# Three changes of place in a hand-ordered scan: one convolution step, the cumulated sums, the residual scaling

## The chip, the core and the metric

One core of one Trainium2 chip. TensorE (PE) multiplies, VectorE (DVE), ScalarE (ACT) and GpSimd (POOL) work element by element, SyncE (SP) issues transfers. The metric is the device time of one execution in microseconds (us).

## The reference

A picture batch of 8 x 128 x 32 x 32 goes through three blocks: attention over the 1024 positions, a state-space scan over the 1024 tokens of each batch element, and a mixture of 8 experts of which each token takes two. The part that the change touches is the scan block. Cut to what matters:

```python
x = x + conv_attention(group_norm(x))
t = tokens(x)
u = rmsnorm(layernorm(t))
z, xBC, dt = split(u @ W_in)                    # 256, 320 and 8 columns
xBC = silu(sum(shift(xBC, k) * conv_w[:, k] for k in range(4)) + conv_b)
xs, Bm, Cm = split(xBC)                         # 256, 32, 32
dt = softplus(dt + dt_bias); dA = exp(dt * -exp(A_log))
state = state * dA + (dt * xs) outer Bm         # one step per token, 8 heads
y = state . Cm + Dp * xs
t = t + layernorm(t) + rmsnorm(y * silu(z)) @ W_out
t = t + experts(layernorm(t))
```

## The kernel before

The kernel has three stages: attention over the eight batch elements, then eight scans (one per batch element, `scanned`), then the experts. Each engine has its own written program; they meet only through semaphores.

A scan handles the 1024 tokens of batch element b in 8 chunks of 128 tokens. Work item n = 8 b + c is chunk c of scan b. In the text "mixed(8)" in a scan means the item of that number counted from the scan's own first chunk, so 8 is the first chunk of the next scan. What one chunk does:

- PE: `decay(n+2)` multiplies the row factors into banks 4 and 5; `out_product(n-2)` is the output projection (L969); `output_rows` (L948, L953, L960) makes y of the chunk; `increments` (L934) runs in chunk 0.
- ACT: `decays(n+2)` takes the exponential of the decay banks (L1341).
- DVE: `mixed(n+1)` multiplies the decays by the inner products (L1805, two inputs in SBUF), `output(n-3)` adds the scaled product into X (L1832), then the chunk's y is gated by z (L1865), `mean_square(n-2)` follows (L1822).
- POOL: `operand` (L531), `root(n-2)`, which takes the power -1/2 of the mean square and releases `output` (L570), and its own parts.

Between these lie the parts that prepare the scans to come. They stand in one list per engine, `pe_parts`, `act_parts`, `dve_parts` and `pool_parts`: which part, how many batch elements ahead, and in which chunk. A place c means after the first step of chunk c on that engine, c + 0.5 the chunk's end, c - 0.25 its start. `slot_of` puts every part of scan 0 one chunk later, at most at 7.5. Parts two elements ahead run in scans 0 to 5, those one ahead in scans 0 to 6.

The parts that matter here:

- The convolution of group g has a first tap on ACT (`tap`, L1272), which reads PE's product of that group, and three steps on DVE, ("conv", (g, k)) for k = 1, 2, 3 (L1713), each adding a shifted row from PSUM to `cacc`. Groups 0 and 1 are xs, group 2 is B and C. The last step raises `m_conv_ready`. Silu on ACT (L1284, L1289) follows in the next scan, where also the gates are multiplied on PE and put through silu on ACT (L1295).
- `softplus` on DVE (L1735 to L1743, two halves) ends with `dec_a` and raises `m_dt_ready`.
- `cumulate` on PE (L881 to L883) sums `dec_a`. It waits for `m_dt_ready` and, as it writes into banks that conv (1,3) reads, for `m_conv_ready` of group 1.
- `exponents` on DVE (L1753 to L1757) reads those sums; `factors` on ACT (L1325, L1328) follows, then PE's first gates, and SP sends the rows through DRAM.
- `shortcut` on ACT (L1258) scales X of one tile of 128 tokens by an instruction; eight make a batch element. Its result is first needed by `output` in the next scan.
- `weighted` on POOL (L561) multiplies xs by the end weights in two parts; the second stands in chunk 6 behind a wait for mixed(7). `decayed` on POOL (L551) stands in chunks 4 and 5. A part on POOL waits for the mix of its chunk first.

Of the kernel before, what the change touches and what calls it, by code (L numbers as in the profile page):

```python
# [16 lines left out]
def hybrid_kernel(nc, x, x_tok, wqk, bqk, wv, bv_rows, wo2, bo, ident, fold, group_mean,  # L17
# [21 lines left out]
    NT = N // P  # L39
# [15 lines left out]
    with ExitStack() as ctx:  # L55
# [598 lines left out]
        def _(pe):  # L654
# [318 lines left out]
            def scan(b, u, first, last):  # L973
                for c in range(NT):
# [31 lines left out]
                    elif c == 7:  # L1006
# [5 lines left out]
            pe_parts = [(gates, (0, 0), 1, 0), (gates, (0, 1), 1, 0), (gates, (1, 0), 1, 0.5), (gates, (1, 1), 1, 0.5), (turn_x, (0,), 1, 2), (turn_x, (1,), 1, 2), (turn_normed, (), 2, 2.5),  # L1012
                        (inner_products, (), 1, 2.5), (group, (0, 0), 2, 3.5), (group, (0, 1), 2, 3.5),
                        (steps, (0, 4), 2, 3.5), (turn_b, (), 1, 3.5), (steps, (4, NT), 2, 4), (group, (1, 0), 2, 4.5),
                        (group, (1, 1), 2, 4.5), (group, (2, 0), 2, 5.5), (group, (2, 1), 2, 5.5), (cumulate, (), 2, 6.5)]

            def pieces(b, slot):
                for part, of, ahead, at in pe_parts:
# [151 lines left out]
        def _(act):  # L1170
# [173 lines left out]
            def scan(b, u, first, last):  # L1344
                for c in range(NT):
# [12 lines left out]
                    elif c == 5:  # L1358
# [3 lines left out]

            act_parts = [(silus, (), 1, 0.5), (normed, (), 2, 1.5), (gather_x, (), 1, 2),
                         (high, (), 2, 2.5), (tap, (0,), 2, 3.5), (gather_b, (), 1, 3.5), (steps, (), 2, 4),
                         (shortcut, (0, 4), 1, 4), (tap, (1,), 2, 4.5), (softplus, (), 2, 4.5), (tap, (2,), 2, 5.5),
                         (shortcut, (4, NT), 1, 5.5), (factors, (), 2, 7)]

            def pieces(b, slot):
                for part, of, ahead, at in act_parts:
# [92 lines left out]
        def _(dve):  # L1462
# [228 lines left out]
            def front(b, u):  # L1691
# [74 lines left out]
                def inner():  # L1766
# [13 lines left out]

            dve_parts = [("conv", (2, 2), 1, -0.25), ("conv", (2, 3), 1, 0), ("ends", (), 1, 1), ("low", (), 2, 2.75),
                         ("inner", (), 1, 3), ("conv", (0, 1), 2, 4), ("conv", (0, 2), 2, 4), ("conv", (0, 3), 2, 4),
                         ("steps", (), 2, 4.5), ("conv", (1, 1), 2, 5), ("conv", (1, 2), 2, 5),
                         ("softplus", (0,), 2, 5.5), ("softplus", (1,), 2, 5.5), ("conv", (1, 3), 2, 6),
                         ("exponents", (), 2, 7), ("conv", (2, 1), 2, 7)]

            def second_front(slot):

# [335 lines left out]
```

## Time and profile before

| what | us |
|---|---|
| median of 3 runs | 956.29 |
| lowest and highest run | 955.75, 958.93 |
| the profiled execution | 954.08 |
| its span, first to last instruction | 952.3 |
| PE busy | 858.4 (90%) |
| DVE busy | 724.0 (76%) |
| ACT busy | 503.3 (53%) |
| POOL busy | 290.8 (31%) |
| all 72 convolution steps on DVE (L1713) | 91.8 |
| all 64 mixed on DVE (L1805) | 85.4 |

The profiled execution's times are those from which single instructions are read; the runs are what the change is measured against. Busy shares are means over three stages. A line of the timeline gives start, duration, engine, source line and operation; a bracket at its end gives how long the engine sat idle before it and what released it.

### The profile page before, as it was taken

How to read it: one execution, taken by the hardware profiler on the slowest of the kernel's cores; microseconds unless marked ns; L12 is line 12 of the kernel's file. 1: busy time of each engine (PE TensorE's matmuls, PEld its weight loads, DVE VectorE, ACT ScalarE, POOL GpSimd, SP SyncE). 2: the span in 40 equal slices, each digit the busy share in tenths (PEclk: the TensorE clock that was granted, in tenths of full speed). 3: DMA queues.
4: the chain of work that ended last, by engine and by line, in shares of the span. 5: the costliest groups of instructions: out<-in, count | busy, mean ns of one | idle time of the engine just before them, and what ended most of it. 6: DMA issues, size and time to landing. Idle time of an engine off the chain costs nothing.

```text
span 952.3 us, 18728 instructions
## 1 busy us (share of the span) xinstructions
PE 858.4 (90%) x7086; PEld 670.9 (70%) x7086; DVE 724.0 (76%) x1959; ACT 503.3 (53%) x740; POOL 290.8 (31%) x264
## 2 busy tenths in 40 slices
PE   3788999999998869898989899899789999999997
PEld 2555556656665758686868777776578898888887
DVE  2867677678767686868687787977968889888885
ACT  1524455455557457566575757464335544555453
POOL 0026110110010236354545454647530333033300
PEclk9979999999999879899999999999899999999999
DMA  5641011011100303213030303041000000000001
GB/s 150 192 143 23 1 23 23 1 23 23 23 1 0 77 4 74 48 31 71 8 76 3 78 1 78 1 96 50 2 1 1 24 23 24 1 23 23 24 2 44
DMA packets 30888, 36.07 MB, mean 38 GB/s; under 512 B 4560, under 2 KB 24912, under 8 KB 30800
## 3 DMA queue, kind: packets, MB, share of 16 engines
q1 hardware_dynamic: 29648, 30.68, 13.2%
q10 hardware_dynamic: 1152, 4.19, 1.2%
q8 instruction: 57, 0.93, 0.4%
q14 instruction: 31, 0.25, 0.1%
HBM read 21.50 MB, written 4.98 MB: 28 GB/s over the span
## 4 chain that ended last, share of the span: by engine, by line
PE 58%; DVE 27%; ACT 7%; issue 5%; POOL 2%; SPq 0%; DMA 0%; DVEq 0%; POOLq 0%; ACTq 0%
PE ps L1047 7%; PE ps L715 6%; DVE cacc L1713 5%; DVE acc L1997 5%; PE ps L702 4%; PE ps L794 3%; PE ps L969 3%; PE ps L796 3%; PE ps L669 3%; PE ps L795 3%; PE ps L674 2%; PE ps L691 2%; PE ps L905 2%; PE ps L684 2%; PE ps L919 2%
## 5 line engine op out<-in xcount | busy, mean ns | idle before, releaser
L1997 DVE SCALAR_TENSOR_TENSOR acc<-ps,comb,acc 128x128 f32<-128x128 f32 x512 | 139.8, 343 | 16.2 <-PE ps L1047 15.6
L1400 ACT ACTIVATE hid<-ps,b_f 128x512 f32<-128x512 f32 x128 | 87.2, 687 | 112.2 <-PE ps L796 112.1
L1047 PEld LDWEIGHTS ps<-w_f,hid 128*128 128x128 f32 x1024 | 130.6, 191 | 19.5 <-ACT hid L1400 8.0
L1047 PE MATMUL ps<-w_f,hid 128*128 128x128 f32 x1024 | 136.8, 277 | 5.0 <-ACT hid L1400 4.5
L1570 DVE TENSOR_REDUCE nmax<-ps 128x1 f32<-128x1024 f32 x64 | 78.1, 1220 | 29.7 <-PE ps L674 29.4
L1713 DVE SCALAR_TENSOR_TENSOR cacc<-ps,cw,cacc 128x1023 f32<-128x1023 f32 (+5 forms) x72 | 91.8, 1275 | 9.4 <-ACT cacc L1272 7.7
L1341 ACT ACTIVATE dcy<-ps 128x1024 f32<-128x1024 f32 x64 | 65.2, 1018 | 62.4 <-PE ps L919 62.3
L570 POOL TENSOR_TENSOR srs<-sve,neg_half 128x1 f32<-128x1 f32 x64 | 58.4, 912 | 117.7 <-DVE gram L1822 117.6
L1187 ACT ACTIVATE probs<-ps,nmax 128x1024 f32<-128x1024 f32 x64 | 71.3, 1113 | 39.2 <-DVE nmax L1570 36.5
L1805 DVE SCALAR_TENSOR_TENSOR dcy<-dcy,g_sb 128x1024 f32<-128x1024 f32 x64 | 85.4, 1334 | 0.3
L702 PEld LDWEIGHTS ps<-id_f,probs 128*128 128x128 f32 x512 | 59.0, 142 | 33.0 <-issue 23.3
L1193 ACT ACTIVATE pt<-ps 128x512 f32<-128x512 f32 x64 | 38.1, 595 | 75.4 <-PE ps L702 74.9
L702 PE MATMUL ps<-id_f,probs 128*128 128x128 f32 x512 | 68.8, 277 | 8.8 <-ACT pt L1193 6.7
L518 POOL TENSOR_TENSOR rs<-bve,neg_half 128x16 f32<-128x16 f32 x8 | 23.2, 2903 | 166.0 <-DVE bve L1618 166.0
L969 PE MATMUL ps<-y_w 128*128 128x256 f32 x256 | 69.4, 395 | 4.9 <-DVE X L1832 4.3
L1575 DVE COPY pt<-ps 128x512 f32<-128x512 f32 x64 | 43.8, 685 | 27.3 <-PE ps L702 27.0
L715 PE MATMUL ps<-pt,v_f 128*64 128x512 f32 x256 | 63.8, 613 | 0.0
L1865 DVE TENSOR_TENSOR y_w<-ps,zs 128x256 f32<-128x256 f32 x64 | 26.9, 420 | 47.8 <-PE ps L960 43.5
L794 PE MATMUL ps<-uh,w_h 128*128 128x512 f32 x128 | 61.1, 478 | 0.0
L1272 ACT ACTIVATE cacc<-ps,cb,cw 128x1024 f32<-128x1024 f32 x24 | 28.9, 1205 | 56.8 <-PE ps L796 56.8
L969 PEld LDWEIGHTS ps<-y_w 128*128 128x128 f32 x256 | 48.2, 194 | 15.2 <-DVE X L1832 5.3
L531 POOL TENSOR_TENSOR xdt<-xs,dts 128x256 f32<-128x256 f32 x64 | 54.0, 848 | 15.6 <-PE ps L960 15.6
(214 smaller groups left out, 1865.3 us busy)
## 6 DMA issues: line engine op xcount, KB each, us to landing
c_dec<-exp_dram SPq DMA_DIRECT2D x32, 256.0 KB, 5.4
xc<-in_x SPq DMA_DIRECT2D x8, 512.0 KB, 3.6
q_b<-q_a SPq DMA_DIRECT2D x16, 256.0 KB, 2.8
X<-in_x_tok ACTq DMA_DIRECT2D x8, 512.0 KB, 5.3
c_rep<-cacc SPq DMA_DIRECT2D x32, 128.0 KB, 4.6
out<-o_ch SPq DMA_DIRECT2D x8, 512.0 KB, 2.6
w_f<-in_w SPq DMA_DIRECT2D x2, 512.0 KB, 4.1
cst_f<-in_sel_rows SPq DMA_DIRECT2D x1, 512.0 KB, 4.4
```

The source lines that it names most:

```text
L702: last = nc.tensor.transpose(T[:, h, k * P:(k + 1) * P], probs[:, j % 2, (4 * h + k) * P:(4 * h + k + 1) * P], id_f[:])
L715: last = nc.tensor.matmul(O[e * DV:(e + 1) * DV, h, :], v_f[u][:, k, :], pt[:, k, h * BANK:(h + 1) * BANK], start=(quarter == 0), stop=(qu ...
L794: nc.tensor.matmul(o, lhs[0], rhs[0], start=True, stop=False)
L969: last = nc.tensor.matmul(ps[:, 6 + n % 2, DI:BANK].rearrange("p (k t) -> p k t", k=2), y_w[:, g, k, :], y_w[:, g, k:5:4 - k, :], start=(g ...
L1047: last = nc.tensor.matmul(ps[:, Y_BANKS[n], t * P:(t + 1) * P], hid[n % 2][:, t * P:(t + 1) * P], w2_f[:, e, :], start=True, stop=True)
L1187: nc.scalar.activation(probs[:, j % 2, :].rearrange("p (a n) -> p a n", a=2), S[j % 2], ACT.Exp, bias=nmax[:, j:j + 1], accum_out=rsum[u][ ...
L1341: nc.scalar.activation(dcy[n % 3][:].rearrange("p (a h) t -> p a (h t)", a=2), ps[:, 4:6, :], ACT.Exp).then_inc(m_decay_ready, 1)
L1400: nc.scalar.activation(hid[n % 2][:], ps[:, 4 + n % 2, :], ACT.Gelu, bias=b1_f[:, n // 2:n // 2 + 1]).then_inc(e_hidden_ready, 1)
L1570: nc.vector.tensor_reduce(nmax[:, j:j + 1], S[j % 2], AX_XY, ALU.max, negate=True).then_inc(max_ready, 1)
L1713: ins = nc.vector.scalar_tensor_tensor(cacc[b % 3][0:rows, g, k:N], banks[:, 0:N - k], cw[0:rows, g, DCONV - 1 - k:DCONV - k], cacc[b % 3] ...
L1805: nc.vector.scalar_tensor_tensor(mix[n % 3][:], dcy[n % 3][:], 1.0, g_sb[u][:, c:c + 1, :].to_broadcast([P, NH, P]), ALU.min, ALU.mult).th ...
L1997: done = nc.vector.scalar_tensor_tensor(acc[u][:, tt, :], ps[:, bank, t * P:(t + 1) * P], comb[u][:, tt, e:e + 1], acc[u][:, tt, :], ALU.m ...
```

## The change

Three lists get other places; no instruction is added, removed or changed in itself.

- DVE: the third step of group 1, ("conv", (1, 3)), moves from chunk 6 to chunk 5, next to the other two. The softplus halves at 5.5 now come behind it.
- PE: `cumulate` moves from the end of chunk 6 (6.5) to chunk 7 (7), where it stands behind that chunk's decay and ahead of its output product. In scan 0 both places become 7.5.
- ACT: `shortcut` is no longer split into tiles 0 to 3 in chunk 4 and 4 to 7 in chunk 5.5; all eight run in chunk 4, ahead of the first tap of group 1 at 4.5.

```diff
-                        (group, (1, 1), 2, 4.5), (group, (2, 0), 2, 5.5), (group, (2, 1), 2, 5.5), (cumulate, (), 2, 6.5)]
+                        (group, (1, 1), 2, 4.5), (group, (2, 0), 2, 5.5), (group, (2, 1), 2, 5.5), (cumulate, (), 2, 7)]
...
-                         (shortcut, (0, 4), 1, 4), (tap, (1,), 2, 4.5), (softplus, (), 2, 4.5), (tap, (2,), 2, 5.5),
-                         (shortcut, (4, NT), 1, 5.5), (factors, (), 2, 7)]
+                         (shortcut, (), 1, 4), (tap, (1,), 2, 4.5), (softplus, (), 2, 4.5), (tap, (2,), 2, 5.5),
+                         (factors, (), 2, 7)]
...
-                         ("steps", (), 2, 4.5), ("conv", (1, 1), 2, 5), ("conv", (1, 2), 2, 5),
-                         ("softplus", (0,), 2, 5.5), ("softplus", (1,), 2, 5.5), ("conv", (1, 3), 2, 6),
-                         ("exponents", (), 2, 7), ("conv", (2, 1), 2, 7)]
+                         ("steps", (), 2, 4.5), ("conv", (1, 1), 2, 5), ("conv", (1, 2), 2, 5), ("conv", (1, 3), 2, 5),
+                         ("softplus", (0,), 2, 5.5), ("softplus", (1,), 2, 5.5), ("exponents", (), 2, 7),
+                         ("conv", (2, 1), 2, 7)]
```

## Rows read from the trace of the kernel before

**Rows 1.** The page, part 4: the ending chain's share of the span by engine.

```profile
PE 58%; DVE 27%; ACT 7%; issue 5%; POOL 2%; SPq 0%; DMA 0%; DVEq 0%; POOLq 0%; ACTq 0%
```

**Rows 2.** Windows: start:end, length, busy (count) by engine, granted clock, DMA; scans 1, 3.

```profile
427.10:474.40 47.30, 43.95 (x477) 35.16 (x476) 35.50 (x69) 29.25 (x43) 22.69 (x23) 0.93 0.21 40
...
518.80:563.10 44.30, 40.92 (x477) 33.24 (x476) 35.49 (x69) 29.23 (x44) 22.66 (x23) 1.00 0.21 43
```

**Rows 3.** The chain in order of time, scan 3: start, us, engine, tile, line.

```profile
518.75 1.21 ACT cacc L1272
519.98 1.29 DVE cacc L1713
...
537.60 1.06 ACT cacc L1289
...
542.87 0.73 PE ps L919 x2
...
563.08 1.22 ACT cacc L1272
```

**Rows 4.** Timeline of DVE, scan 3, chunk 5 to the next chunk 0.

```profile
519.98 2.60 DVE L1713 SCALAR_TENSOR_TENSOR cacc<-ps,cw,cacc 128x1023 f32<-128x1023 f32 x2
...
525.50 1.22 DVE L1805 SCALAR_TENSOR_TENSOR dcy<-dcy,g_sb 128x1024 f32<-128x1024 f32 x1
...
526.89 1.27 DVE L1713 SCALAR_TENSOR_TENSOR cacc<-ps,cw,cacc 128x1021 f32<-128x1021 f32 x1
...
528.62 1.22 DVE L1805 SCALAR_TENSOR_TENSOR dcy<-dcy,g_sb 128x1024 f32<-128x1024 f32 x1
530.28 0.35 DVE L1832 SCALAR_TENSOR_TENSOR X<-ps,srs,X 128x128 f32<-128x128 f32 x1 [0.44 <-POOL srs L570]
...
534.48 1.65 DVE L1805 SCALAR_TENSOR_TENSOR dcy<-dcy,g_sb 128x1024 f32<-128x1024 f32 x1
```

**Rows 5.** Timeline of PE: its waits before cumulate and gates, scans 0, 1, 3.

```profile
392.24 0.41 PE L881 MATMUL ps<-dec_a,tri_f 128*128 128x64 f32 x2 [1.85 <-DVE cacc L1713]
...
394.72 0.77 PE L794 MATMUL ps<-xh,w_zh 128*128 128x512 f32 x1 [0.83 <-ACT expc L1328]
...
436.67 0.41 PE L881 MATMUL ps<-dec_a,tri_f 128*128 128x64 f32 x2 [2.15 <-DVE cacc L1713]
...
528.30 0.41 PE L881 MATMUL ps<-dec_a,tri_f 128*128 128x64 f32 x2 [2.13 <-DVE cacc L1713]
```

**Rows 6.** Timeline of ACT: residual scaling and the tap behind it.

```profile
559.18 1.64 ACT L1258 ACTIVATE X<-X,rnb,rp 128x128 f32<-128x128 f32 x4
563.08 1.21 ACT L1272 ACTIVATE cacc<-ps,cb,cw 128x1024 f32<-128x1024 f32 x1 [2.25 <-PE ps L796]
```

**Rows 7.** Timeline of POOL, scan 3, chunk 6.

```profile
526.98 1.48 POOL L561 TENSOR_TENSOR xw<-xs,wend 128x768 f32<-128x768 f32 x1 [2.52 <-DVE dcy L1805]
528.78 1.47 POOL L570 TENSOR_TENSOR srs<-sve,neg_half 128x1 f32<-128x1 f32 x1 [0.31 <-DVE gram L1822]
```

**Rows 8.** Timeline of DVE, scan 6, chunks 5 to 7.

```profile
649.08 2.63 DVE L1805 SCALAR_TENSOR_TENSOR dcy<-dcy,g_sb 128x1024 f32<-128x1024 f32 x1
...
652.96 2.26 DVE L1805 SCALAR_TENSOR_TENSOR dcy<-dcy,g_sb 128x1024 f32<-128x1024 f32 x1
655.67 0.35 DVE L1832 SCALAR_TENSOR_TENSOR X<-ps,srs,X 128x128 f32<-128x128 f32 x1 [0.44 <-POOL srs L570]
```

**Rows 9.** Timeline of POOL, the same stretch of scan 6.

```profile
648.55 2.09 POOL L551 TENSOR_TENSOR c_dec<-c_dec,c_rep 128x896 f32<-128x896 f32 x1
...
652.67 1.47 POOL L561 TENSOR_TENSOR xw<-xs,wend 128x768 f32<-128x768 f32 x1
```

**Rows 10.** Timeline of DVE, scan 0: exponents behind cumulate.

```profile
393.27 0.23 DVE L1753 COPY ein<-ps 128x64 f32<-128x64 f32 x1 [0.64 <-PE ps L883]
```

**Rows 11.** Windows, columns as in rows 2: two stretches of low clock.

```profile
394.50:402.00 7.50, 7.28 (x87) 6.03 (x88) 5.42 (x9) 6.24 (x7) 0.11 (x1) 0.57 0.27 68
...
438.20:442.30 4.10, 4.10 (x42) 2.95 (x40) 2.27 (x6) 1.44 (x3) 0.40 (x1) 0.58 0.08 19
```

## The prediction

> **What bounds the kernel now.** The page comes first: the chain that ended last is 58% PE and 27% DVE [rows 1], a mean over three stages, so it says nothing about one edit. The diff touches only the lists that place work in the chunks of the eight scans (about 338 to 700 us), so I cut that stage into one window per scan, from one first tap of group 1 to the next. An undisturbed scan, such as scan 3, lasts 44.30 us at a granted clock of 1.00; scan 1 lasts 47.30 us at 0.93 [rows 2]. Then I read the chain inside scan 3 [rows 3]. It is a ring of three arcs. The first tap of group 1 on ACT starts at 518.75. From 519.98 the chain is DVE work, from conv (1,1) to conv (2,3), until the group's silu starts on ACT at 537.60. ACT (silu, gates, table load, decay) hands over to PE at 542.87, and PE runs with hardly a gap until the next tap at 563.08. So a scan is 17.6 us of DVE, 5.3 us of ACT, and 21.4 us of PE and the tap that follows.
>
> In the DVE arc the rows follow one another without a gap, but for 0.44 us before the output row at 530.28 [rows 4]. PE, in the same stretch, sits idle for 2.13 us ahead of cumulate at 528.30, released by conv (1,3) [rows 5]. That wait is what the eye falls on and what this change takes away. But the DVE arc does not wait for cumulate: its result is first read by exponents, behind the output row at 530.28, 2 us after cumulate starts. So PE idles there because it is ahead, and time won there is not time of the scan.
>
> **conv (1,3) from chunk 6 to chunk 5.** Nothing is added or removed. One instruction of 1.27 us [rows 4] goes from behind mixed(7) to ahead of the chunk's gating; a repeat of it costs half of the pair's 2.60, 1.30 us. It is moved past gating(5), mean_square(3), both softplus halves, mixed(7) and output(3), which all come 1.30 us later; what follows its old place keeps its time, so far. Five scans have this (1 to 5), scan 0 one chunk later in another company, scans 6 and 7 have no fronts left to build. Who waits for the delayed ones: cumulate now starts when softplus ends, and PE's output product in chunk 7 waits for output(3). mixed(7) ended at 525.50 + 1.22 = 526.72 and will end at 528.02. PE's rows of chunk 7 need it, and come no later than before, for they stood behind a cumulate that began at 528.30.
>
> What decides is the neighbour. POOL's weighted, second part, is released by mixed(7): it started at 526.98, 0.26 us behind mixed(7)'s end, and took 1.48 us [rows 7]. Before, conv (1,3) stood between mixed(7) and the next mixed, so weighted was over (528.46) when mixed(8) started at 528.62 with 1.22 us [rows 4, 7]. After, only output(3), gating(6) and mean_square(4) stand between: mixed(8) starts at 528.62 + 1.30 - 1.27, about 528.65, while weighted runs from 528.28 to 529.76. Scan 6 has no convolutions, and its chunk 6 is this order: weighted from 652.67 to 654.14, mixed from 652.96, and that mixed takes 2.26 us instead of 1.22, ending 1.08 us after weighted [rows 8, 9]. One chunk earlier a mixed beside decayed takes 2.63 us and ends 1.07 us after it [rows 8, 9]. So mixed does not share with POOL; it does its work when POOL's instruction is through. Then root runs until mixed has ended, and output(4) starts at 655.67, 1.53 us behind weighted's end [rows 8].
>
> The sum for one scan: mixed(7)'s end to output(4) was 530.28 - 526.72 = 3.56 us, conv (1,3) among it. After, it is 0.26 + 1.48 + 1.53 = 3.27: taking conv (1,3) out of this stretch wins only 0.29, and putting it ahead of mixed(7) costs 1.30. The difference is 1.0 us. All of it is in the DVE arc, ahead of exponents and conv (2,1) to (2,3), so on the chain; ACT's factors, the row DMAs and the silu of the group move with it. Five scans: +5.0 us. The bounds of one collision: 0.43, the smallest excess of a mixed that met POOL work late (1.65 against 1.22 at 534.48 [rows 4]), and 1.41, the largest (2.63 against 1.22). Five times that is +2.2 to +7.1. I take 1.0, because the row it comes from is the same pair of instructions in the same order.
>
> **Scan 0.** Its slots are one chunk later and cumulate stays where it was. Here exponents really waited for cumulate, 0.64 us at 393.27 [rows 10]; with conv (1,3) a chunk earlier cumulate depends on softplus, which ends before gating(7), so most of this goes: -0.5 us (between 0 and -0.64). weighted runs beside exponents and conv (2,1) there, which are no mixed; a conv beside weighted took its usual 1.27 us [rows 4, 7].
>
> **cumulate behind decay in chunk 7.** Three pairs of matmuls change places with two. The decay no longer waits behind cumulate, whose own wait now holds back the output product and the rows of chunk 7. In scan 3 cumulate would start near 526.9 (softplus's end, 525.5 + 1.3), ahead of the old 528.30, so nothing behind it comes later. Cost nothing; cover: the DVE arc, which reads the product about 2 us later.
>
> **shortcut whole in chunk 4 (ACT).** Eight scalings in one go instead of four and four: 1.64 us more ahead of the first tap of group 1, which is on the chain. ACT was idle for 2.25 us there [rows 6], so 0.6 us of cover is left, and each tenth beyond it would be paid six times. 1.64 us less lie behind the second tap, so the decay of chunk 8 on ACT comes that much sooner; the decay behind it on PE needs this to go ahead of cumulate. mixed(8) never waited for it. In scan 6 the same move pushes one decay, whose readers there are held by POOL (the 2.63 us). Cost nothing.
>
> **The clock.** Where PE's waits go matters for its clock. After the 2.15 us wait in scan 1 [rows 5] the granted clock fell to 0.58 for 4.1 us, after scan 0's waits of 1.85 and 0.83 us to 0.57 for 7.5 us [rows 5, 11]; in scans 2 to 5, of which scan 3 stands here, the same wait left it at 1.00 [rows 2]. Scan 1 holds two such stretches, one of them behind no long wait, and is 3.0 us longer than scan 3 [rows 2], 1.5 us each. After the change PE is about 1.4 us ahead in chunk 7 (cumulate near 526.9 instead of 528.30) and waits instead in the next chunk 0, by estimate about 1 us before the gates (factors come 1.0 us later) and 1 us before increments (output(5) does). I take no change in the number of stretches, as the sum of the waits is about the same, and keep both sides as rivals.
>
> Sum: 954.08 us for the profiled execution (span 952.3) + 5.0 - 0.5 = 958.6. The median of the runs shown is 956.29, 2.2 us above that execution; the changed kernel is timed like the runs, so 956.29 + 4.5 = 960.8 us.
>
> **Rivals.** (a) PE's wait is time of the scan: if somewhere in the DVE arc a hidden wait for PE were given back, the change would win up to 2.13 us in five scans and the 0.64 of scan 0, 11.3 us: 945.0. It decides if mixed(8) starts at 527.4 and conv (2,3) with it comes earlier than before. For it: the largest wait of PE in these scans. Against it: no idle row in front of any DVE instruction there but 0.44, by POOL. Chance 0.13.
>
> (b) The long wait of PE is cut into shorter ones and the clock no longer falls: scan 1's 3.0 us are won, and in scan 0, at 1.5 us for 4.1, up to 2.7 for its 7.5: 960.8 - 5.7 = 955.1, no change. For it: two of the three stretches stand behind long waits. Against it: four scans with the same wait kept the clock. The same case holds smaller collisions near the lower bound. Chance 0.22. The Trainium skill, page "TensorE: Matmul & The Clock Gate", section "HAM oscillation — how this bites in real kernels", says that a wait long enough lets the clock fall, again and again in a loop that waits each time; by that rule shorter waits would keep it, and the result would be (b)'s.
>
> (c) The new waits fall close together and the clock falls in every scan: 1.5 us in five scans on top, 968.3. For it: scan 0's two waits, 1.85 and 0.83 us, had the longest stretch behind them. Chance 0.10. The same page's section "A second HAM failure mode: psum-queue depth-cycling" describes a clock that swings under frequent short idles; no row here shows short idles alone doing that.
>
> (d) The forecast: +4.5, chance 0.55.
>
> **How the numbers follow.** A measurement of this kernel can tell about 0.3%, 2.9 us, from no change. The forecast alone spans +1.6 (2.2 - 0.64) to +7.1, 957.9 to 963.4; a tenth of its chance falls below +2.9. Slower 0.50 + 0.10 = 0.60; same 0.05 + 0.22 = 0.27; faster 0.13. To hold 8 in 10 the range takes in (b) at its lower end and one or two clock stretches more at the upper: 955.0 to 966.0.
>
> **What would show it.** Right: cumulate's idle of 2.1 us is gone in scans 1 to 5; mixed(8) there takes 1.9 to 2.3 us beside weighted; undisturbed scans last 45.3 us instead of 44.3, with more idle of PE at the head of each scan; the first tap of group 1 keeps some 0.6 us of idle before it. Wrong: if mixed(8) keeps 1.22 us; if scans last 44.3 or less; if the tap is late; or if the clock row differs by more than one stretch from before.

## The result and the profile after

The changed kernel takes 961.91 us (median of 16 runs, 958.46 to 964.28); the kernel before takes 956.85 us beside it (16 runs, 952.63 to 959.96). The ratio is 1.0048 with a 95% interval of 1.0032 to 1.0065, which is 3.1 to 6.2 us: slower, by 5.1 us in the medians, and by more than the 0.3% that counts. The forecast was 960.8 us. Its profiled execution took 962.57 us, with a span of 960.8.

One window per scan, from one first tap of group 1 to the next (start:end, length, busy time and count of PE, PEld, DVE, ACT and POOL, granted clock, DMA share, GB/s). Scans 0 to 4 of the kernel after:

```profile
387.16:430.83 43.67, 40.89 (x435) 32.83 (x434) 32.75 (x64) 28.23 (x43) 19.19 (x21) 0.92 0.21 43
430.83:476.02 45.19, 41.43 (x477) 33.12 (x476) 36.43 (x69) 29.16 (x44) 22.76 (x23) 1.00 0.21 42
476.02:521.20 45.18, 41.43 (x477) 33.12 (x476) 36.41 (x69) 29.15 (x44) 22.73 (x23) 1.00 0.19 41
521.20:567.97 46.77, 43.01 (x477) 34.17 (x476) 36.41 (x69) 29.14 (x43) 22.74 (x23) 0.96 0.20 40
567.97:613.18 45.21, 41.47 (x477) 33.12 (x476) 36.42 (x69) 29.15 (x44) 22.74 (x23) 1.00 0.20 42
```

The reader is to see two things. Undisturbed scans (clock 1.00) last 45.18 to 45.21 us, against 44.30 to 44.33 before [rows 2]: 0.88 us more each. And scan 3, which was undisturbed before, now holds a stretch at half clock (the lower of the two levels of PE's clock, 1.2 of 2.4 GHz) and lasts another 1.6 us. The stretch stands near the scan's end: the granted clock is 0.57 from 562 to 566 us and 1.00 from the scan's start to 562. Meanwhile scan 1, which lasted 47.30 us before [rows 2], is free of it.

The chain of waits in scan 3 of the kernel after (start, length, engine, tile, line), which answers to [rows 3]:

```profile
529.13 1.23 DVE dcy L1805
...
530.62 1.48 POOL xw L561
532.10 1.50 POOL srs L570
533.62 0.03 DVE X L1832
```

Before, DVE worked from the first convolution step to the last with hardly a gap but for 0.44 us [rows 4]. The profile's chain of the kernel before does not stay on DVE all that way, though. In the part that [rows 3] leaves out it goes through cumulate on PE and comes back at conv (2,1):

```profile
528.30 0.41 PE ps L881 x2
...
531.40 1.20 DVE cacc L1713
```

The reason is gating(7), which needs PE's rows of chunk 7 (L960). PE's timeline and DVE's there:

```profile
531.79 0.65 PE L960 MATMUL ps<-dcy,xdt 128*32 128x128 f32 x16
```

```profile
532.62 0.42 DVE L1865 TENSOR_TENSOR y_w<-ps,zs 128x256 f32<-128x256 f32 x1
```

The rows end at 532.44, and conv (2,1), which stands ahead of gating(7) on DVE, ends at 532.59. So PE's way through cumulate, its wait included, ended 0.15 us ahead of DVE's own: two ways of nearly one length lay side by side. After the change the rows end at 533.41 and gating(7) starts at 535.96, so this way now has some 2.5 us to spare.

Now the chain leaves DVE behind mixed(7), runs through weighted and root on POOL, and comes back at output(4). The timelines of DVE and POOL show the same place (start, length, engine, line, operation, tiles; in brackets the idle time before, and who ended it). DVE, answering to [rows 4]:

```profile
522.43 3.92 DVE L1713 SCALAR_TENSOR_TENSOR cacc<-ps,cw,cacc 128x1023 f32<-128x1023 f32 x3
526.27 0.41 DVE L1865 TENSOR_TENSOR y_w<-ps,zs 128x256 f32<-128x256 f32 x1
...
529.13 1.22 DVE L1805 SCALAR_TENSOR_TENSOR dcy<-dcy,g_sb 128x1024 f32<-128x1024 f32 x1
...
531.07 2.11 DVE L1805 SCALAR_TENSOR_TENSOR dcy<-dcy,g_sb 128x1024 f32<-128x1024 f32 x1
533.62 0.35 DVE L1832 SCALAR_TENSOR_TENSOR X<-ps,srs,X 128x128 f32<-128x128 f32 x1 [0.45 <-POOL srs L570]
```

POOL, answering to [rows 7]:

```profile
530.62 1.48 POOL L561 TENSOR_TENSOR xw<-xs,wend 128x768 f32<-128x768 f32 x1 [2.52 <-DVE dcy L1805]
532.05 1.53 POOL L570 TENSOR_TENSOR srs<-sve,neg_half 128x1 f32<-128x1 f32 x1
```

mixed(8) starts 0.45 us after weighted, takes 2.11 us instead of 1.22, and ends at 533.18, which is 1.08 us behind weighted's end (532.10). That distance is the one of scan 6 before [rows 8, 9]. From mixed(7)'s end (530.35) to output(4) it is 3.27 us; before it was 3.56, with conv (1,3) among it.

What became of the wait that the change took away? PE's timeline of scan 3, answering to [rows 5]:

```profile
529.27 0.43 PE L881 MATMUL ps<-dec_a,tri_f 128*128 128x64 f32 x2
530.66 1.13 PE L969 MATMUL ps<-y_w 128*128 128x256 f32 x4 [0.38 <-DVE X L1832]
535.34 0.47 PE L794 MATMUL ps<-xh,w_zh 128*128 128x512 f32 x1 [1.26 <-ACT expc L1328]
539.83 0.99 PE L934 MATMUL ps<-xw,b_tok 128*32 128x64 f32 x56 [0.97 <-issue]
```

Cumulate (L881) has no idle before it. Where 2.13 us stood there are now 0.38, 1.26 and 0.97 us, 2.61 in all, in other places.

How the 8.5 us between the two profiled executions (962.57 - 954.08) are made up: the first tap comes 4.19 us later (387.16 against 382.97), in a stretch that the change hardly touches, at a granted clock of 0.93 against 0.95; the five windows add 1.61 (226.02 against 224.41); the rest of the span adds 2.7, of which scan 5 has the same collision (mixed(8) takes 2.11 us there too, about 0.9) and the scans' last stretch, 44 to 45 us long, has a granted clock of 0.88 against 0.92. So one execution against one shows the loss mixed with clock; the windows at 1.00 show it alone. By those it is 5 x 0.88 - 0.46 (scan 0, 43.67 against 44.13, with a granted clock of 0.92 in both) = 3.9 us. The medians differ by 5.1; 3.9 lies inside the interval of 3.1 to 6.2, so what the other 1.1 us are is not shown. The median granted clock is 0.961 over the 16 runs after, and 0.963 to 0.965 over the groups of runs of the kernel before that stand beside the experiments: in the direction of a loss, but hardly apart.

### The profile page after: what moved, and what is told of

Its sections match the earlier page's. It is cut to its first block, busy times and chain, and to the rows that moved or that the text cites. A ratio compares the mean times of both kernels' runs of the same rounds, so it can differ in the third digit from the quotient of the medians.

```text
span 960.8 us, 18728 instructions
## 1 busy us (share of the span) xinstructions
PE 865.8 (90%) x7086; PEld 674.0 (70%) x7086; DVE 724.7 (75%) x1959; ACT 502.7 (52%) x740; POOL 290.0 (30%) x264
## 3 DMA queue, kind: packets, MB, share of 16 engines
q10 hardware_dynamic: 1152, 4.19, 1.2%
## 4 chain that ended last, share of the span: by engine, by line
PE 57%; DVE 26%; ACT 6%; issue 6%; POOL 3%; SPq 0%; DMA 0%; DVEq 0%; POOLq 0%; ACTq 0%
PE ps L1047 7%; PE ps L715 6%; DVE acc L1997 5%; DVE cacc L1713 5%; PE ps L702 4%; PE ps L794 3%; PE ps L796 3%; PE ps L795 3%; PE ps L669 3%; PE ps L969 3%; PE ps L674 2%; PE ps L691 2%; PE ps L905 2%; PE ps L684 2%; PE ps L725 2%
## 5 line engine op out<-in xcount | busy, mean ns | idle before, releaser
L1805 DVE SCALAR_TENSOR_TENSOR dcy<-dcy,g_sb 128x1024 f32<-128x1024 f32 x64 | 89.8, 1404 | 0.3
L969 PE MATMUL ps<-y_w 128*128 128x256 f32 x256 | 71.7, 405 | 5.6 <-DVE X L1832 4.9
L1865 DVE TENSOR_TENSOR y_w<-ps,zs 128x256 f32<-128x256 f32 x64 | 26.8, 419 | 50.3 <-PE ps L960 47.7
L607 POOL TENSOR_TENSOR ers<-eve,neg_half 128x8 f32<-128x8 f32 x8 | 14.1, 1759 | 145.0 <-DVE eve L1912 145.0
```

The lines of the kernel that those rows point to most:

```text
L969: last = nc.tensor.matmul(ps[:, 6 + n % 2, DI:BANK].rearrange("p (k t) -> p k t", k=2), y_w[:, g, k, :], y_w[:, g, k:5:4 - k, :], start=(g ...
L1805: nc.vector.scalar_tensor_tensor(mix[n % 3][:], dcy[n % 3][:], 1.0, g_sb[u][:, c:c + 1, :].to_broadcast([P, NH, P]), ALU.min, ALU.mult).th ...
```

## Experiments

Every kernel below was timed against the kernel before on the same chip. The range in brackets behind a ratio is its 95% interval; "scan lengths" are those of scans 0 to 4 from tap to tap in the profile of one execution.

### e1: conv (1,3) alone moved, in the kernel before

```diff
-                         ("steps", (), 2, 4.5), ("conv", (1, 1), 2, 5), ("conv", (1, 2), 2, 5),
-                         ("softplus", (0,), 2, 5.5), ("softplus", (1,), 2, 5.5), ("conv", (1, 3), 2, 6),
+                         ("steps", (), 2, 4.5), ("conv", (1, 1), 2, 5), ("conv", (1, 2), 2, 5), ("conv", (1, 3), 2, 5),
+                         ("softplus", (0,), 2, 5.5), ("softplus", (1,), 2, 5.5),
```

> The kernel before with one edit: conv (1,3) in chunk 5; cumulate and shortcut stay. Theory (mixed(8) meets the second part of weighted on POOL): the whole loss comes with this edit, +4 to +5 us over before, mixed(8) near 2.1 us in scans 1 to 5, undisturbed scans about 45.2 us. Rival (the loss is cumulate behind decay, or the tap behind eight scalings): no loss here, within 1.5 us of before.

Measured: 961.39 us against 956.84, ratio 1.0055 (1.0038 to 1.0072). Scan lengths 43.67, 45.18, 46.68, 45.18, 45.20. DVE's timeline in scan 3 has the same collision as the kernel after:

```profile
526.65 1.22 DVE L1805 SCALAR_TENSOR_TENSOR dcy<-dcy,g_sb 128x1024 f32<-128x1024 f32 x1
...
528.59 2.12 DVE L1805 SCALAR_TENSOR_TENSOR dcy<-dcy,g_sb 128x1024 f32<-128x1024 f32 x1
```

The whole loss is that one instruction's place. The two other edits, on top of it, change neither the length of an undisturbed scan (45.18 us in both) nor the median (961.39 against 961.91) by more than the runs can tell.

### e2: the other two edits alone

In the kernel after, conv (1,3) goes back to chunk 6; cumulate stays behind decay and the residual scaling whole.

```diff
-                         ("steps", (), 2, 4.5), ("conv", (1, 1), 2, 5), ("conv", (1, 2), 2, 5), ("conv", (1, 3), 2, 5),
-                         ("softplus", (0,), 2, 5.5), ("softplus", (1,), 2, 5.5), ("exponents", (), 2, 7),
-                         ("conv", (2, 1), 2, 7)]
+                         ("steps", (), 2, 4.5), ("conv", (1, 1), 2, 5), ("conv", (1, 2), 2, 5),
+                         ("softplus", (0,), 2, 5.5), ("softplus", (1,), 2, 5.5), ("conv", (1, 3), 2, 6),
+                         ("exponents", (), 2, 7), ("conv", (2, 1), 2, 7)]
```

> The changed kernel with conv (1,3) back in chunk 6; cumulate in chunk 7 and shortcut whole remain. Theory: within 1.5 us of before, mixed(8) 1.22 us, undisturbed scans 44.3 us, the first tap of group 1 keeps about 0.7 us of idle. Rival: the loss of 4 to 5 us is here. If the wait of 2.1 us on PE were time of the scan, some of it would be won here too, as the decay no longer stands behind it.

Measured: 962.28 us against 956.84, ratio 1.0040 (1.0016 to 1.0064): a miss. DVE has no collision (mixed(8) takes 1.22 us), and yet the scan lengths are 44.12, 45.22, 46.92, 45.27, 46.92. PE's timeline, and windows over two scans and over the 5 us around cumulate:

```profile
486.21 0.41 PE L881 MATMUL ps<-dec_a,tri_f 128*128 128x64 f32 x2 [1.49 <-DVE cacc L1713]
487.14 2.08 PE L969 MATMUL ps<-y_w 128*128 128x256 f32 x4
...
493.33 1.02 PE L969 MATMUL ps<-y_w 128*128 128x256 f32 x4
```

```profile
431.00:476.00 45.00, 42.38 (x477) 33.87 (x476) 35.33 (x68) 29.27 (x43) 22.49 (x23) 0.96 0.21 42
476.00:521.00 45.00, 42.33 (x457) 34.07 (x455) 34.64 (x64) 28.98 (x43) 22.49 (x22) 0.93 0.20 42
486.00:491.00 5.00, 4.79 (x38) 3.77 (x42) 4.02 (x11) 0.42 (x2) 1.83 (x2) 0.66 0.03 7
```

Behind the wait of 1.49 us the same output product takes 2.08 us instead of 1.02, and the granted clock is 0.66 over 5 us; scans 1 to 4 all have such a stretch there, and scans 2 and 4 a second one near their end. PE's rows come late, and gating(7) waits 1.07 us in scan 2. So in this execution the two edits have no price in DVE's own work, but one through PE's clock. It is the slowest of the ten, which run from 954.73 to 965.24 us; the median granted clock over them is 0.956 against 0.963, but what the faster ones look like inside is not on record.

### e6 and e7: each of those two edits alone, in the kernel before

```diff
 e6:
-                         (group, (1, 1), 2, 4.5), (group, (2, 0), 2, 5.5), (group, (2, 1), 2, 5.5), (cumulate, (), 2, 6.5)]
+                         (group, (1, 1), 2, 4.5), (group, (2, 0), 2, 5.5), (group, (2, 1), 2, 5.5), (cumulate, (), 2, 7)]
 e7:
-                         (shortcut, (0, 4), 1, 4), (tap, (1,), 2, 4.5), (softplus, (), 2, 4.5), (tap, (2,), 2, 5.5),
-                         (shortcut, (4, NT), 1, 5.5), (factors, (), 2, 7)]
+                         (shortcut, (), 1, 4), (tap, (1,), 2, 4.5), (softplus, (), 2, 4.5), (tap, (2,), 2, 5.5),
+                         (factors, (), 2, 7)]
```

> The kernel before with only cumulate moved behind decay in chunk 7. The pair of PE and ACT edits ran 4 us slower at a lower mean clock (0.956 against 0.963) with its DVE rows unchanged. Theory: the cost is PE's clock after the waits in chunk 7, so this edit alone shows it: a mean clock under 0.960 and 2 to 5 us over before, and at equal clock the same time as before. Rival: the shortcut edit makes it; then this one is within 1.5 us of before.

> The kernel before with only shortcut whole in chunk 4. Theory: within 1.5 us of before, mean clock near 0.963, the first tap of group 1 keeps 0.7 us of idle. Rival: 2 to 5 us slower.

Measured, e6: 953.19 us against 957.02, ratio 0.9957 (0.9938 to 0.9975), faster where e2 had let me expect slower: a miss. Scan lengths 44.02, 44.29, 44.32, 44.31, 44.30. e7: 956.08 us, ratio 0.9998 (0.9983 to 1.0014); scan lengths 44.14, 47.27, 44.33, 44.29, 44.29, the pattern of the kernel before.

e6 tells two things apart. PE's timeline in its scan 2, and a window over scan 1:

```profile
481.37 0.74 PE L919 MATMUL ps<-rhs_c,lhs_c 128*128 128x512 f32 x2 [0.80 <-ACT dcy L1341]
482.72 0.41 PE L881 MATMUL ps<-dec_a,tri_f 128*128 128x64 f32 x2 [0.61 <-DVE cacc L1713]
```

```profile
431.00:475.00 44.00, 40.89 (x476) 32.96 (x472) 35.23 (x69) 28.96 (x44) 22.39 (x23) 1.00 0.22 43
```

The 2.13 us in one piece have become 0.80 and 0.61, and 0.57 more stand ahead of increments. An undisturbed scan still lasts 44.3 us: with the wait in pieces no time comes back, which is what the forecast held against rival (a). In the profile e6 gains in scan 1, 44.3 us at full clock instead of 47.3: that is rival (b)'s mechanism, seen without the collision. But this execution is no faster than the profiled one of before as a whole (954.87 against 954.08 us), because it loses some 4 us outside these scans. That the 3.8 us between the medians come from such scans is not shown; the median granted clock (0.968 against 0.965) points that way. Between e6 and e2 only the residual scaling differs. With it whole, ACT's decays come early, the 0.80 us in front of the decay go, and PE waits 1.49 us at cumulate in one piece; then the clock falls. With it in halves PE waits 1.41 us in two pieces and the clock holds. That is one execution of each.

### e3 and e9: weighted moved out of the way

If the collision is the cause, the loss must go when POOL's second part of weighted starts behind mixed(8). The slot 7.5 puts it there. e3 does it in the kernel after, e9 in the kernel before as a control.

```diff
-                          (weighted, (1,), 6.5)]
+                          (weighted, (1,), 7.5)]
```

> The changed kernel with the second part of weighted on POOL at 7.5 instead of 6.5, so behind mixed(8). Theory: mixed(8) takes 1.22 us again, output(4) starts about 2.4 us behind mixed(7)'s end instead of 3.27, scans 1 to 5 win 0.9 us each and the kernel comes to before's time, less the 0.5 us of scan 0: about 4.5 us faster than the changed kernel, ratio to before 0.998 to 1.001. Rival (the displacement of softplus, mixed(7) and cumulate by 1.2 us is what costs, whatever POOL does): no faster than the changed kernel, 1.004 to 1.006.

> The kernel before with only the second part of weighted at 7.5. There it met no mixed in scans 1 to 5, so by the theory nothing is won: undisturbed scans 44.3 us, ratio 0.998 to 1.002. If putting weighted later helped for another reason, this kernel would win the 8 us that it won against the changed kernel.

Measured, e3: 953.08 us against 956.84, ratio 0.9970 (0.9951 to 0.9990). Scan lengths 43.65, then four between 44.27 and 44.31. DVE and POOL in scan 3:

```profile
527.84 1.22 DVE L1805 SCALAR_TENSOR_TENSOR dcy<-dcy,g_sb 128x1024 f32<-128x1024 f32 x1
529.50 0.35 DVE L1832 SCALAR_TENSOR_TENSOR X<-ps,srs,X 128x128 f32<-128x128 f32 x1 [0.44 <-POOL srs L570]
```

```profile
528.00 1.46 POOL L570 TENSOR_TENSOR srs<-sve,neg_half 128x1 f32<-128x1 f32 x1 [3.13 <-DVE gram L1822]
529.44 1.48 POOL L561 TENSOR_TENSOR xw<-xs,wend 128x768 f32<-128x768 f32 x1
```

mixed(8) is back at 1.22 us and the scan at 44.3. Cumulate does not wait at all in these scans, as in the kernel after, and they still last what they lasted before. Against the kernel after e3 wins 8.8 us in the medians, where 4.5 were expected; 0.9 us a scan are the collision, and scans 1 to 4 hold no stretch at half clock. e9: 956.81 us against 957.71, ratio 0.9993 (0.9975 to 1.0012), with undisturbed scans of 44.30. In the order of before conv (1,3) had kept the two apart, so there was nothing to win. The pair shows that the 0.9 us a scan of e3 over the kernel after are the collision and not the place of weighted as such.

### e8: the collision doubled

Both parts of weighted at 6.5, in the kernel after.

```diff
-            pool_parts = [(weighted, (0,), 2.5), (totals, (), 3.5), (decayed, (0,), 4.5), (decayed, (1,), 5.5),
-                          (weighted, (1,), 6.5)]
+            pool_parts = [(totals, (), 3.5), (decayed, (0,), 4.5), (decayed, (1,), 5.5),
+                          (weighted, (0,), 6.5), (weighted, (1,), 6.5)]
```

> The changed kernel with both parts of weighted at 6.5, so about 3.4 us of POOL work instead of 1.5 released by mixed(7). Theory (mixed(8) does its work when weighted is through): mixed(8) takes about 4.0 us instead of 2.1 in scans 1 to 5, and each scan, scan 6 too, is 1.9 us longer: 9 to 12 us over the changed kernel, near 972. Rival (the loss is not weighted's): no change against the changed kernel.

Measured: 973.25 us against 957.02, ratio 1.0164 (1.0129 to 1.0199). Scan lengths 41.97, 46.77, 47.72, 47.76, 47.80: scans 2 to 4 are 2.55 us longer than an undisturbed one of the kernel after. The direction and about the size were expected, the manner was not. DVE and POOL in scan 2:

```profile
484.01 1.22 DVE L1805 SCALAR_TENSOR_TENSOR dcy<-dcy,g_sb 128x1024 f32<-128x1024 f32 x1
...
485.94 2.55 DVE L1805 SCALAR_TENSOR_TENSOR dcy<-dcy,g_sb 128x1024 f32<-128x1024 f32 x1
490.37 0.35 DVE L1832 SCALAR_TENSOR_TENSOR X<-ps,srs,X 128x128 f32<-128x128 f32 x1 [1.88 <-POOL srs L570]
```

```profile
485.50 4.33 POOL L561 TENSOR_TENSOR xw<-xs,wend 128x1024 f32<-128x1024 f32 x2 [2.53 <-DVE dcy L1805]
489.79 0.54 POOL L570 TENSOR_TENSOR srs<-sve,neg_half 128x1 f32<-128x1 f32 x1
```

The two parts of weighted one by one (shortest, median and longest in ns, first and last start):

```profile
L561 POOL TENSOR_TENSOR xw<-xs,wend x2: 1912/2187/2462, 485.5 to 487.4; 128x1024 f32<-128x1024 f32 x1, 128x768 f32<-128x768 f32 x1
```

mixed(8) does not wait for both. It waits for the first part (1.91 us) and does its work between the two; the second part, alone 1.48 us, then takes 2.46 us because it waits for mixed. Output(4) pays either way: it needs root, which stands behind weighted on POOL, and starts 5.14 us behind mixed(7)'s end (485.23) instead of 3.27, so 1.87 us of the 2.55 are the collision. (That mixed(8) takes 2.55 us as well is chance.) The other 0.68 us are not taken apart; they go with PE's clock: PE waits 3.13 us for the late factors, the granted clock is 0.66 over the next 10 us, and the silu of the gates, L1295, waits 0.91 us for PE. PE's first gates, and the window behind that wait:

```profile
492.09 0.77 PE L794 MATMUL ps<-xh,w_zh 128*128 128x512 f32 x1 [3.13 <-ACT expc L1328]
```

```profile
490.00:500.00 10.00, 7.91 (x91) 6.51 (x92) 8.79 (x17) 6.57 (x8) 3.09 (x6) 0.66 0.42 96
```

### e4, e5 and e10: what is next on the arc, and a version faster than both

The rows of before hold another mixed that meets POOL work, mixed(9) with 1.65 us [rows 4], between conv (2,2) and conv (2,3). The silu of group 2 waits for conv (2,3); in the kernel after, ACT idles 1.53 us for it. e4 is e3 with that mixed behind conv (2,3), in chunk 0 of scans 1 to 6; e5 is this edit alone in the kernel before.

```diff
+                    late_mix = c == 0 and 0 < b < B - 1
-                    if n + 1 < NT * B:
+                    if n + 1 < NT * B and not late_mix:
                         mixed(n + 1)
                     if n >= 3:
                         output(n - 3)
...
                     pieces(b, c)
+                    if late_mix:
+                        mixed(n + 1)
```

> As the kernel with weighted at 7.5, and in chunk 0 of scans 1 to 6 mixed stands behind output(5) and conv (2,3) instead of ahead of them. Theory (the DVE arc sets the scan): conv (2,3) ends about 1.6 us sooner; in the changed kernel ACT stood idle 1.53 us ahead of the group's silu, so up to 1.5 us a scan is won, six scans: 5 to 9 us under before, ratio 0.990 to 0.995. If PE's increments or gates bind instead: within 2 us of the kernel with weighted at 7.5 alone.

> The kernel before with only the edit of chunk 0: in scans 1 to 6 mixed stands behind output(5) and conv (2,3). If the DVE arc alone sets the scan: 1.6 us a scan, six scans, 0.990. Theory (in the kernel before ACT reaches the group's silu only 0.1 us ahead of conv (2,3), so ACT binds next): under 2 us, 0.998 to 1.000. Then the gain of the order with mixed last needs PE and ACT ahead, which is what cumulate behind decay gives.

Measured, e4: 949.63 us against 956.84, ratio 0.9926 (0.9902 to 0.9949), the fastest of all. Windows of its scans 1 and 4, then DVE and ACT in scan 3:

```profile
429.54:473.83 44.29, 42.85 (x477) 34.03 (x476) 35.06 (x69) 29.13 (x43) 22.65 (x23) 0.96 0.22 42
...
562.35:605.10 42.75, 41.31 (x477) 33.08 (x476) 35.04 (x69) 29.12 (x43) 22.65 (x23) 1.00 0.21 44
```

```profile
535.31 1.21 DVE L1805 SCALAR_TENSOR_TENSOR dcy<-dcy,g_sb 128x1024 f32<-128x1024 f32 x1
```

```profile
533.45 2.00 ACT L1284 ACTIVATE cacc<-cacc 128x1024 f32<-128x1024 f32 x2
535.42 1.06 ACT L1289 ACTIVATE cacc<-cacc 64x1024 f32<-64x1024 f32 x1
```

Both effects are there: mixed(9) alone takes 1.21 us, and the silu of group 2 (L1289) follows that of the other groups without idle time. An undisturbed scan lasts 42.75 us, 1.53 less than in e3. Scans 1 to 3 hold a stretch at half clock each, near their end (granted clock 0.57 from 468 to 472 us in scan 1), and last 44.2 to 44.3. No wait of PE in that scan 1 is over 0.39 us; no run here shows what brings the stretch on.

e5: 961.50 us against 957.02, ratio 1.0029 (1.0008 to 1.0049), a miss: I had expected no change or a small gain. Scan lengths 44.15, 45.61, 45.67, 45.64, 47.20. PE still waits 2.15 us ahead of cumulate, the granted clock from 486 to 492 us, the stretch behind it, is 0.72, and PE's rows of chunk 7 (L960) end only at 492.24. Gating(7) on DVE waits until then (the bracket names no releaser, but the rows' end fits):

```profile
492.37 0.43 DVE L1868 TENSOR_TENSOR y_w<-ps,zs 128x256 f32<-128x256 f32 x1 [1.57 <-issue]
```

In scan 1 of the kernel before, with its half-clock stretch behind cumulate, the same gating waits 1.52 us; in scan 3, at full clock, the rows came 0.15 us ahead. So that near tie is where a slow PE behind cumulate costs time. The edit that is worth 1.5 us a scan in e4 is lost behind a slower PE in e5; every scan of e5 holds a half-clock stretch, so what the edit is worth there at full clock is not shown. (L1868 is the gating, L1865 of before, three lines further down in e4, e5 and e10.)

e10 goes one step on from e4: conv (2,1) ahead of mixed(8), at 6.75, so that root has time to finish and the 0.44 us before output(4) go.

```diff
-                         ("softplus", (0,), 2, 5.5), ("softplus", (1,), 2, 5.5), ("exponents", (), 2, 7),
-                         ("conv", (2, 1), 2, 7)]
+                         ("softplus", (0,), 2, 5.5), ("softplus", (1,), 2, 5.5), ("conv", (2, 1), 2, 6.75),
+                         ("exponents", (), 2, 7)]
```

> As the kernel with mixed last in chunk 0, and conv (2,1) at 6.75, between mean_square(4) and mixed(8), so that root is through before mixed begins. Theory (mixed and POOL exclude each other): output(4) no longer waits its 0.44 us in scans 1 to 5, about 2 us won; in scan 0 exponents come behind conv (2,1), up to 1.3 us lost: 0 to 2 us under the kernel it starts from. Rival (the 0.44 is root's own run time): no change, or 1 us worse.

Measured: 954.13 us against 957.71, ratio 0.9968 (0.9946 to 0.9990); faster than before, but slower than e4, which was not expected. The 0.44 us are gone as meant. An undisturbed scan, however, lasts 43.53 us instead of 42.75:

```profile
515.98:559.51 43.53, 41.15 (x477) 33.15 (x476) 34.99 (x69) 29.13 (x43) 20.32 (x23) 1.00 0.23 43
```

ACT's timeline, first in e10, then in e4:

```profile
529.45 0.26 ACT L1325 ACTIVATE eo<-ein 128x64 f32<-128x64 f32 x1 [4.30 <-DVE ein L1757]
...
532.08 2.01 ACT L1284 ACTIVATE cacc<-cacc 128x1024 f32<-128x1024 f32 x2
```

```profile
530.81 0.26 ACT L1325 ACTIVATE eo<-ein 128x64 f32<-128x64 f32 x1 [3.52 <-DVE ein L1757]
```

Counted from the scan's first tap (515.98 in e10, 518.14 in e4), factors start at 13.47 in e10 and at 12.67 in e4, 0.80 us later. In e4 the arc no longer runs through conv (2,1) to (2,3), it runs through exponents to factors, a table load and the silu on ACT, without idle time. conv (2,1), 1.27 us, now stands ahead of exponents and wins 0.44 there: +0.83, and the scans measure +0.78. Scan 0, where conv (2,1) also comes first, lasts 44.36 us against 43.63 in e4. The expectation had still counted with e3's arc.

## Why the forecast was right, step by step

**DVE's arc is the ring's second part, and the wait of PE is not.** Right in what it came to. Output(4) and what follows moved by the collision alone (e1, e3), and in e3, where cumulate does not wait and mixed(8) takes 1.22 us, a scan still lasts 44.3 us. Rival (a), 945.0 us, is out: mixed(8) started no earlier (9.87 us behind the scan's first tap, before and after), and conv (2,3) came later. The reading it rested on was too simple, though. The chain was not DVE work alone from conv (1,1) to conv (2,3): it ran through cumulate and PE's rows, from 528.30 to 531.40. The tightest reader of what stood behind PE's wait was gating(7), with 0.15 us to spare, and not exponents. No time was to be won there because DVE's own way was as long; but the forecast did not see how near PE's was, and so not why a half-clock stretch behind cumulate costs time (1.52 us in scan 1).

**The collision.** Right in its place, its kind and its size: mixed(7)'s end to output(4) was put at 3.27 us and took 3.27; mixed(8) was to take 1.9 to 2.3 us and took 2.11. The Trainium skill, page "SBUF — State Buffer", section "Who interferes with whom", has a rule for this: a VectorE instruction with two inputs in SBUF contends with a GpSimd instruction that reads SBUF, over ports that one of them holds exclusively, and a VectorE instruction with at most one such input does not, unless it runs in a mode that uses both ports. The trace agrees: mixed ends 1.08 us behind weighted, and e8 shows the exclusion from both sides (2.55 us for mixed, 2.46 us for the second part of weighted), while convolution steps, with one input in SBUF, take 1.28 us beside POOL's decayed (522.50 to 524.60 in the kernel after) and 1.27 with POOL idle (at 531.32 in the kernel before).

**conv (1,3)'s new place.** The term that was mis-sized, by a little. It was put at 1.30 us, half of the pair; from the tap to gating(5) it is 5.07 us after (521.20 to 526.27) and 3.87 before, so 1.20. Less 0.29 that makes 0.91, and the scans show 0.88 instead of 1.0. Five scans: 4.4 instead of 5.0.

**Scan 0.** Put at -0.5, measured 43.67 against 44.13, -0.46. The wait of exponents for cumulate, 0.64 us, is gone. Both windows hold half-clock stretches (0.92), at different places, so the last tenth is not to be trusted.

**cumulate at nothing, shortcut at nothing.** Right on top of conv (1,3): the kernel after and e1 agree within 0.5 us. The cover was as estimated: the tap behind the whole residual scaling has 0.70 us of idle left, 0.6 was said. But as a statement on the edits alone it was too simple. Alone, cumulate's move gains 3.8 us (e6), and with the scaling whole it loses 5.4 (e2), in medians; in the profiles the difference between them is PE's clock.

ACT's timeline after, the residual scaling and the tap, answering to [rows 6]:

```profile
517.32 3.18 ACT L1258 ACTIVATE X<-X,rnb,rp 128x128 f32<-128x128 f32 x8
521.20 1.20 ACT L1272 ACTIVATE cacc<-ps,cb,cw 128x1024 f32<-128x1024 f32 x1 [0.70 <-PE ps L796]
```

**The clock.** "No change in the number of stretches" held in the five windows: three before and three after, at other places. Scan 0 has two short ones instead of one long (granted clock 0.92 in both kernels), scan 1 lost both of its own (0.93 to 1.00), scan 3 has one (1.00 to 0.96). Outside the windows they grew (0.95 to 0.93 ahead of them, 0.92 to 0.88 in the scans' last stretch). PE's new waits, put at about 1 us before gates and 1 us before increments, are 1.26 and 0.97. Rival (c) did not come about: with those two waits scans 1, 2 and 4 stayed at 1.00, and the stretch in scan 3 begins some 22 us behind the second of them, so neither wait explains it. Rival (b)'s mechanism shows in e3 and e6, whose scans 1 to 4 are all at 1.00 and which run 3.8 us under the kernel before; and scan 1 of the kernel after is free of its two stretches. Its 3.0 us were won there, and lost again at other places. Why the stretches came at those places is open.

The 4.5 us of the forecast are thus 3.9 us in windows at full clock. The medians differ by 5.1 us, with an interval of 3.1 to 6.2, and the 1.1 us between are within that. That the total came within 1.1 us of 960.8 is in part luck: single runs of one kernel lie up to 7 us apart, and the clock term, put at nothing, is not known to better than that interval.

## What to carry to other kernels

An instruction between two others can be what keeps them from colliding on another engine: before moving it, look at who starts in its old place on each engine that shares something with it, and price the collision from a spot of the trace where the two already meet. An idle wait of the engine with the most work is only time if what it delivers late is read at once, and if no other way of the same length stands beside it. Here the profile's chain ran through the 2.1 us of PE, and filling them gained nothing on the ring, because DVE's way was as long; so look first at who reads the result, when, and what else that reader waits for. After each step that works, find the arc anew before taking the next (e10): the operation that was on it may not be any more.

## What the runs showed of the hardware

The exclusion between mixed and POOL's instructions acts per instruction and in both directions, the one that comes later waits: in e8 mixed slips in between two POOL instructions that stand back to back, and the second of them is stretched from 1.48 to 2.46 us. Even root, of 128 x 1 elements, takes 1.46 to 1.53 us beside a mixed and 0.55 alone.

PE's waits go with a lower clock at some places and not at others, and not by their length alone. A wait of 2.13 to 2.15 us leaves the granted clock at 1.00 in scans 2 to 5 of the kernel before and is followed by a stretch at half clock in scan 1; one of 1.49 us is followed by such a stretch in scans 1 to 4 of the one profiled execution of e2; 0.80 and 0.61 us, with matmuls between, leave it at 1.00 in e6. The Trainium skill, page "TensorE: Matmul & The Clock Gate", section "HAM oscillation — how this bites in real kernels", has a loop's long wait lower the clock each time round; e2 looks like that, the kernel before, with the longer wait, mostly does not. Other stretches stand behind no such wait: scan 1 of e4 has one from 468 to 472 us, and no wait of PE in it is over 0.39 us. What decides stays open; no run here separates the possible reasons. What is shown is the price: a scan with one such stretch lasts 0.9 us longer (scan 1 of e2) to 1.6 us longer (scan 3 of the kernel after), and runs of one kernel differ by some 7 us (952.63 to 959.96 before), so edits of this size are best read from single scans at a granted clock of 1.00.
